# Second cross attention: norms and gate by ScalarE, statistics over three slots, last batch finished by halves

## What is computed

```python
def _L1_xattn_ref(x, latents, mask, kv_gate, ...):       # x: context [4, 1601, 256], latents: tokens [4, 512, 256]
    x = layernorm(x, gamma_media, beta_media)
    latents = layernorm(latents, gamma_lat, beta_lat)
    kv = concatenate((x, latents * kv_gate), axis=1)      # 2113 keys
    q, k, v = latents @ Wq, kv @ Wk, kv @ Wv              # 8 heads of 64
    sim = einsum(q * SCALE, k); sim = sim - max(sim)
    attn = softmax(where(valid, sim, -1e30))
    return einsum(attn, v) @ Wout
x = _layernorm(x + _L1_xattn_ref(ctx, x, mask, ...))      # then the experts, which first choose 2 of 8 by x @ gate_w
```

## Time and profile before

| | |
|---|---|
| median of 3 runs | 2418.3 us (2417.81 to 2419.02) |
| the profiled execution | 2418.87 us, its span 2417.1 us |
| busy | PE 2027.0, DVE 1616.6, ACT 1121.6, POOL 938.3 us |
| second cross attention | about 909 to 2057 us of the span |
| units 1 to 32, from one L2137 to the next | 968.9 to 2003.4 us |
| mean granted TensorE clock | 0.926 of full speed |

### The profile page before, as it was taken

One profiled execution on the slowest core, in us unless ns is written; L12 is line 12 of the kernel. 1 busy time (PEld: TensorE's weight loads), 2 busy tenths in 40 slices (PEclk: granted clock), 3 DMA queues, 4 the chain that ended last, 5 costly groups with the idle time before them and its releaser, 6 DMA issues. The chain is left out here.

```text
span 2417.1 us, 35796 instructions
## 1 busy us (share of the span) xinstructions
PE 2027.0 (84%) x12728; PEld 1406.0 (58%) x12728; DVE 1616.6 (67%) x2541; ACT 1121.6 (46%) x2142; POOL 938.3 (39%) x728
## 2 busy tenths in 40 slices
PE   7889849978899965877899799988899986599993
PEld 4556639962344444554566565655566564499992
DVE  5687745445878874888888877888788884322224
ACT  3333211103744653656666476656676672133332
POOL 3233232323113200455576456564576572222222
PEclk9999969988999987989999899999999998699997
DMA  3110035210000002000000000000000000531113
GB/s 148 37 37 21 10 144 206 91 57 18 1 1 1 0 1 90 1 1 1 28 1 1 10 28 1 1 10 1 1 1 1 10 1 9 221 134 36 38 34 113
DMA packets 36714, 93.29 MB, mean 39 GB/s; under 512 B 5415, under 2 KB 24379, under 8 KB 31934
## 3 DMA queue, kind: packets, MB, share of 16 engines
q1 hardware_dynamic: 30462, 74.72, 8.6%
q0 software_dynamic: 6080, 16.29, 2.0%
HBM read 76.56 MB, written 14.44 MB: 38 GB/s over the span
## 5 line engine op out<-in xcount | busy, mean ns | idle before, releaser
L1965 POOL TENSOR_TENSOR x_total<-x_total,x_pt 128x1024 f32<-128x1024 f32 x186 | 439.2, 2361 | 198.4 <-ACT x_pt L2024 182.4
L2045 ACT ACTIVATE x_pt<-PS,x_maskf 128x512 f32<-128x512 f32 x544 | 332.2, 687 | 180.8 <-PE PS L2313 177.8
L2127 DVE TENSOR_TENSOR PS<-x_pt,PS 128x512 f32<-128x512 f32 x480 | 333.2, 694 | 74.8 <-ACT x_pt L2045 36.8
L2284 PE MATMUL PS<-x_pt,x_vs 128*64 128x256 f32 x2176 | 286.1, 404 | 77.9 <-ACT x_pt L2024 72.1
L2145 DVE TENSOR_TENSOR x_pt<-x_pt,PS 128x1024 f32<-128x1024 f32 x320 | 320.4, 1051 | 0.7 <-PE PS L2331 0.7
L2024 ACT ACTIVATE x_pt<-x_pt 128x1536 f32<-128x1536 f32 (+1 forms) x160 | 266.1, 1664 | 50.6 <-DVE x_pt L2145 50.4
L2313 PE MATMUL PS<-x_qs,x_ks 64*128 64x256 f32 x2176 | 282.0, 395 | 1.9 <-ACT x_pt L2045 1.9
L2284 PEld LDWEIGHTS PS<-x_pt,x_vs 128*64 128x64 f32 x2176 | 153.8, 143 | 205.8 <-ACT x_pt L2024 78.0
L1143 PEld LDWEIGHTS PS<-m_xT,m_own 128*128 128x128 f32 x1984 | 235.5, 195 | 7.4 <-DVE m_own L1219 3.3
L1143 PE MATMUL PS<-m_xT,m_own 128*128 128x128 f32 x1984 | 236.4, 278 | 3.2 <-DVE m_own L1219 2.8
L2313 PEld LDWEIGHTS PS<-x_qs,x_ks 64*128 64x128 f32 x2176 | 199.5, 189 | 65.7 <-issue 40.2
(11 more groups left out here) (269 smaller groups left out, 2861.1 us busy)
## 6 DMA issues: line engine op xcount, KB each, us to landing
f_w<-in_L_ffn_w SPq DMA_DIRECT2D x32, 1024.0 KB, 6.3
a_ctxT<-in_ctxT SPq DMA_DIRECT2D x8, 800.5 KB, 4.4
f_w<-ys SPq DMA_DIRECT2D x24, 256.0 KB, 5.9
x_cx<-in_ctx SPq DMA_DIRECT2D x4, 1536.0 KB
l_w<-in_L_attn_w SPq DMA_DIRECT2D x6, 512.0 KB
a_xT<-in_xT SPq DMA_DIRECT2D x4, 512.0 KB, 5.2
X<-in_x SPq DMA_DIRECT2D x1, 2048.0 KB, 11.1
xr<-a_xn SPq DMA_DIRECT2D x16, 128.0 KB, 1.7
```

The source lines that it names most:

```text
L1965: ins = nc.gpsimd.tensor_tensor(total2[:], first, tile[:, 2 * k + 2:2 * k + 4, :], ALU.add)
L2045: nc.scalar.activation(pt[:, s % 2, t, :].rearrange("p (h n) -> p h n", h=2), PS[:, first:first + 2, half], ACT.Identity, bias=maskf[:, b ...
L2127: ins = nc.vector.tensor_tensor(acc, tile, acc, ALU.max)
L2284: mm = nc.tensor.matmul(PS[h * HDX:(h + 1) * HDX, AVB, 0:QN], vs[:, p % 2, t, h * HDX:(h + 1) * HDX], pt[:, u % 2, t, h * QN:(h + 1) * QN] ...
```

## The change

1. Norms by ScalarE. For b >= 1 `normalise` and the norm of the finished rows are ACT Identity activations with bias = -mean x rstd and scale = rstd, at the end of ACT's work of a group, in the same slots 3 and 4 (finished rows: slot 3, gi = 4). Batch 0's first norm stays with DVE. POOL's `rstd` and `rstd_out` get two small instructions each, for the bias.
2. `gate` is two ACT Copy activations, right behind the last N move (slot 6, gi = 4).
3. `stats` and `aggregate` go to slots 0, 1 and 2: 6, 6 and 5 tiles.
4. The loop ends with slot 32. What follows is written out: `weigh(31)` goes to bank 2, group by group as exponentials come; POOL adds up tiles 0 to 9 of unit 31 and PE the last 7; the O products are taken apart (`last_product`), with pairs 0 to 2 ahead of the last unit; residual, norm, transpose and logits go by halves, in banks of their own.

```diff
-        SLOTS = range(-1, UNITS + 6)
+        SLOTS = range(-1, UNITS + 1)
+        FINAL_AVB, FINAL_OUT, FINAL_TURN, FINAL_LOGITS = 2, (RB, 0), (1, 3), (ACC, AVB)
+        POOLED = 10
+                nc.gpsimd.tensor_scalar(nmu[:], mv[:, :, 0], -1.0, None, ALU.mult).then_inc(negated, 1)
                 pool.wait_ge(eps_added, b + 1)
+                if b >= 1:
+                    pool.wait_ge(ln_ready, b * NS)
                 nc.gpsimd.tensor_tensor(rs[:], ve[:], g["mhalf"][:].to_broadcast([P, NS]), ALU.pow).then_inc(rs_ready, 1)
+                pool.wait_ge(rs_ready, b + 1)
+                pool.wait_ge(negated, b + 1)
+                nc.gpsimd.tensor_tensor(shift[:], nmu[:], rs[:], ALU.mult).then_inc(shift_ready, 1)
...
+            u = UNITS - 1
+            for k in range(POOLED // 2 - 1):
+                add_up(u, k)
+            pool.wait_ge(summed, u * SUMS + POOLED // 2 - 1)
+            pool.wait_ge(av_done, u * NG)
+            nc.gpsimd.tensor_tensor(total[:], total2[:, 0, :], total2[:, 1, :], ALU.add).then_inc(summed, 1)
+            for half in range(2):
+                at = slice(2 * half, 2 * half + 2)
+                pool.wait_ge(mv2_ready, J * (B - 1) + 2 * half + 2)
+                nc.gpsimd.tensor_scalar(ve2[:, at], mv2[:, at, 1], LN_EPS, None, ALU.add).then_inc(eps2_added, 1)
+                pool.wait_ge(eps2_added, B + half)
+                nc.gpsimd.tensor_tensor(rs2[:, at], ve2[:, at], g["mhalf"][:].to_broadcast([P, 2]), ALU.pow).then_inc(rs2_ready, 1)
...
+                if use[0] == "N" and use == last_turn(use[1]):
+                    gate(use[1])
+
+            def gate(b):
+                act.wait_ge(moved, MOVED[last_turn(b)])
+                for k in range(KD):
+                    ins = nc.scalar.activation(kvT[:, b % 2, k, S2:KEYS], latT[:, k, :], ACT.Copy, scale=cols[:, 4 * KD:4 * KD + 1])
+                ins.then_inc(gated, 1)
+
+            def normalise(b, i):
+                src, dst, np_ = source(b, i)
+                if i == 0:
+                    act.wait_ge(shift_ready, b + 1)
+                nc.scalar.activation(dst, src, ACT.Identity, bias=shift[0:np_, i:i + 1], scale=rs[0:np_, i:i + 1])\
+                    .then_inc(ln_ready, 1)
...
+                    if exists(s) and s // UB + 1 < B and s % UB in (3, 4):
+                        at = (s % UB - 3) * NG + gi - 1
+                        for k in (2 * at, 2 * at + 1):
+                            if 0 <= k < NS:
+                                normalise(s // UB + 1, k)
+                    if UB <= s < UNITS and s % UB == 3 and gi == 4:
+                        b = s // UB
+                        act.wait_ge(shift2_ready, b)
+                        for j in range(J):
+                            x = X[:, (b - 1) * J + j, :]
+                            nc.scalar.activation(x, x, ACT.Identity, bias=shift2[:, j:j + 1], scale=rs2[:, j:j + 1])\
+                                .then_inc(x5_ready, 1)
+
+            exponent(UNITS - 1, NG - 1)
+            for half in range(2):
+                act.wait_ge(last_turned, half + 1)
+                if half == 0:
+                    act.wait_ge(ring_done, USE[("L", B - 2, 1)] + 1)
+                else:
+                    act.wait_ge(last_logits, 1)
+                nc.scalar.copy(x5T[:].rearrange("p j k n -> p (j k n)"), PS[:, FINAL_TURN[half], :]).then_inc(last_moved, 1)
...
+                avb = FINAL_AVB if u == UNITS - 1 else AVB
                 dve.wait_ge(av_done, u * NG + NG)
...
+            STATS = {at: range(at * NS // 14, (at + 1) * NS // 14) for at in range(14)}
-            dve.wait_ge(w_loaded, 16 * 6)
-            gate(0)
...
+                        for k in STATS.get(i * NG + gi, ()):
+                            counted[b + 1, k] = stats(b + 1, k)
+                        for k in STATS.get(i * NG + gi - 1, ()):
+                            aggregate(b + 1, k, counted[b + 1, k])
...
+            def last_residual(half):
+                dve.wait_ge(last_out, half + 1)
+                for i in range(2):
+                    x = X[:, (B - 1) * J + 2 * half + i, :]
+                    nc.vector.tensor_tensor(x, PS[:, FINAL_OUT[half], i * D:(i + 1) * D], x, ALU.add).then_inc(last_read, 1)
+                for i in range(2):
+                    j = 2 * half + i
+                    dve.wait_ge(last_read, 2 * half + i + 1)
+                    link(nc.vector.bn_stats(bn2[:, j, :], X[:, (B - 1) * J + j, :]))
+                    nc.vector.bn_aggr(mv2[:, j, :], bn2[:, j, :]).then_inc(mv2_ready, 1)
+
+            def last_norm(half):
+                dve.wait_ge(rs2_ready, B + half)
+                for j in (2 * half, 2 * half + 1):
+                    x = X[:, (B - 1) * J + j, :]
+                    nc.vector.tensor_scalar(x, x, mv2[:, j, 0:1], rs2[:, j:j + 1], ALU.subtract, ALU.mult).then_inc(x5_ready, 1)
+
+            def last_choice(half):
+                dve.wait_ge(last_logits, half + 1)
+                first = (B - 1) * J + 2 * half
+                nc.vector.tensor_copy(LG[:, first:first + 2, :],
+                                      PS[:, FINAL_LOGITS[half], 0:2 * E].rearrange("p (j e) -> p j e", e=E)).then_inc(LG_ready, 1)
+
+            last_residual(0)
+            weighted(UNITS - 1)
+            last_norm(0)
+            last_residual(1)
+            last_choice(0)
+            last_norm(1)
+            last_choice(1)
+            dve.wait_ge(LG_ready, 2)
...
+            def last_product(half, pairs):
+                for i in range(2):
+                    j = 2 * half + i
+                    for p in pairs:
+                        mm = nc.tensor.matmul(PS[:, FINAL_OUT[half], i * D:(i + 1) * D], o[:, p, j * P:(j + 1) * P], wo[:, p, :],
+                                              start=(i == 0 and p == 0), stop=(i == 1 and p == PAIRS_X - 1))
+                if pairs[-1] == PAIRS_X - 1:
+                    mm.then_inc(last_out, 1)
...
+                    if s == UNITS and gi == 0:
+                        released(pe, BY_NUMBER[-1])
+                        last_product(0, (0, 1, 2))
+                        pe.wait_ge(s_moved, UNITS * KT)
+                        last_product(1, (0, 1))
...
+            u = UNITS - 1
+            b, p, hq = unit(u)
+            pe.wait_ge(o_ready, u - 1)
+            last_product(1, (2,))
+            for gi in range(NG):
+                pe.wait_ge(exp_done, u * NG + gi + 1)
+                released(pe, ("V", b, p, gi))
+                for t in TILES[gi]:
+                    for h in range(2):
+                        nc.tensor.matmul(PS[h * HDX:(h + 1) * HDX, FINAL_AVB, 0:QN], vs[:, p % 2, t, h * HDX:(h + 1) * HDX],
+                                         pt[:, u % 2, t, h * QN:(h + 1) * QN], start=(t == 0), stop=False)
+            for t in range(POOLED, KT):
+                for h in range(2):
+                    nc.tensor.matmul(PS[h * HDX:(h + 1) * HDX, FINAL_AVB, QN:2 * QN], ones[:, 0:HDX],
+                                     pt[:, u % 2, t, h * QN:(h + 1) * QN], start=False, stop=False)
+            pe.wait_ge(o_ready, u)
+            last_product(0, (3,))
+            pe.wait_ge(summed, u * SUMS + POOLED // 2)
+            for h in range(2):
+                mm = nc.tensor.matmul(PS[h * HDX:(h + 1) * HDX, FINAL_AVB, QN:2 * QN], ones[:, 0:HDX],
+                                      total[:, h * QN:(h + 1) * QN], start=False, stop=True)
+            mm.then_inc(av_done, NG)
+            pe.wait_ge(o_ready, UNITS)
+            last_product(1, (3,))
+            for half in range(2):
+                pe.wait_ge(x5_ready, J * (B - 1) + 2 * half + 2)
+                for i in range(2):
+                    for k in range(KD):
+                        mm = nc.tensor.transpose(PS[:, FINAL_TURN[half], (i * KD + k) * P:(i * KD + k + 1) * P],
+                                                 X[:, (B - 1) * J + 2 * half + i, k * P:(k + 1) * P], ident[:])
+                mm.then_inc(last_turned, 1)
+                pe.wait_ge(last_moved, half + 1)
+                for i in range(2):
+                    for k in range(KD):
+                        mm = nc.tensor.matmul(PS[:, FINAL_LOGITS[half], i * E:(i + 1) * E], x5T[:, i, k, :], wg[:, k, :],
+                                              start=(k == 0), stop=(k == KD - 1))
+                mm.then_inc(last_logits, 1)
```

More of the change, by code:

```diff
@@ L2287, in weigh @@
                                                       start=(t == 0), stop=False)
[L2288 to L2294 removed]
+                        if gi == NG - 1:
                             pe.wait_ge(summed, (u + 1) * SUMS)
```

51 lines of the change are left out of this document (16 added, 35 removed).

## The result

The changed kernel takes 2316.1 us (median of 4 runs, 2314.09 to 2318.73) against 2418.66 us of the kernel before on the same chip (4 runs): ratio 0.9576, 95% interval 0.9564 to 0.9587. Its profiled execution took 2316.37 us with a span of 2314.6, so 102.5 us less span than before (2417.1). The forecast was 2320.6 us, its range 2298 to 2352.

What follows compares the result with a forecast made beforehand. An odd slot was taken to last as long as DVE's list plus the turn of the maxima through PE. Terms of 54.1 + 4.8 + 21.9 - 3.3 + 0 - 0.3 + 20.5 = 97.7 us gave 2320.6 us, range 2298 to 2352.

Steps and rivals of the forecast that it cites:

- slots 3 and 4, batches 0 to 2: Norms moved from DVE to ACT in these slots: 236.6 us become 182.5, 54.1 us gained.
- slots 27 and 28: Batch 3, where only the finished rows' norm leaves DVE: 63.09 us become 58.3, 4.8 gained (1 to 6).
- gate, slots 7: Gate ready before slot 7 begins: three slots fall from 34.6 to 27.3 us each, 21.9 gained (12 to 23).
- the end, with slot 31's 1.4: After the last exponential: last logits copied at 2036.4 instead of 2056.9, 20.5 us gained (14 to 24).
- the choice between the bounds: Slots 3 and 4, batches 0 to 2: gain from 30.6 us to 65.5; a value nearer the upper end taken.
- the rival in which all of it lies on the path: ACT becomes the bound, all its added work on the path: 25.5 us less gain, 2346 us; chance 0.22.
- 1.1 a slot, near two of 0.592: Slot 6: the gate's two ACT activations ahead of the score moves cost 1.1 us each slot, 3.3 lost (0 to 7).
- I charge 2 x 2.5 lost and 3 x 1.6 gained: Statistics: slots 0 of batches 1 and 2 lose 2.5 us each, slots 1 gain 1.6; net 0 (-5 to +5).
- not counted: the higher clock in slots that follow a pause: Slots that followed a pause before the change: a higher clock there, left out of the sum, no size given.
- The rival that PE works at half clock there: The end keeps its length: PE at half clock in the last 25 us, gain 10 not 20.5, 2331 us; chance 0.10.
- the case of all hidden: Rival: ACT's added work fully hidden, statistics in slot 0 free: 118.8 us gained, 2299.5 us; chance 0.13.
- The slower case: Rival: PE at half clock for whole slots 3 and 4, 27.7 us a slot; 2487 with all six; chance 0.04.

Runs made afterwards that it cites:

- e8: Changed kernel with a second ACT activation of the same size behind each of the 51 context and token norms, into a spare tile: 2334.85 us, 18.8 longer.
- e7: Changed kernel with ACT's context and token norms cut from 256 to 16 columns in batches 1 to 3: 2310.31 us, 5.8 shorter.
- e2: Changed kernel with the statistics put back to slots 1 and 2 of a batch, two tiles a group: 2323.21 us, 7.1 longer.
- e3: Kernel before with only the new end (and POOL's small bias operations, unused): 2402.19 us, 17.3 faster than before.
- e1: Changed kernel with the gate alone given back to DVE, at the start of slot 7: 2337.88 us, 21.8 longer.
- e10: Changed kernel with transposes and logits of the finished rows' second half moved from slot 5 to slot 7: 2306.65 us, 9.8 shorter.

## Why the prediction was right, point by point

The forecast of the sum was 97.7 us, the span shows 102.5. By terms, from the windows of the kernel before and of the two profiles of the changed kernel:

| term | forecast | measured | second profile |
|---|---|---|---|
| slots 3 and 4, batches 0 to 2 | 54.1 | 55.9 (236.6 to 180.8) | 52.6 |
| slots 27 and 28 | 4.8 | 4.9 | 4.9 |
| gate, slots 7 | 21.9 | 22.5 | 22.5 |
| gate, slots 6 | -3.3 | 0.0 | 0.0 |
| statistics, slots 0 to 2 | 0 | 3.6 | 4.0 |
| slots 5, batches 1 and 2 | not counted | -5.1 | -3.4 |
| start | -0.3 | -1.2 | 0.2 |
| the end, with slot 31's 1.4 | 20.5 | 21.5 | 20.5 |

The two columns of one program show how finely the terms can be read: to about 3 us for slots 3 and 4, to 1.6 for slots 5, to 1.4 for the start. Of slots 3 and 4 and of slots 5, 1.9 us is only the moved mark: cut at PE's turn of the maxima they are 54.0 and -3.2 (50.7 and -1.6 in the second profile).

*The reading of the bound held.* An odd slot lasts as long as DVE's list and the turn: slot 11 with DVE at 24.02 lasts 27.45 us. The price of ACT's norm (0.592 from the earlier trace rows, 0.60 to 0.62 measured) held, and so did the choice between the bounds. The split was a little off: slots 3 came at 27.5 instead of 28.4, since ACT's rest in the later groups was larger than the 2.3 us taken (in e8 eight activations more, 4.9 us, made these slots only 1.9 longer); slots 12 and 20 at 35.4 and 33.8 instead of 33.5, and at 35.3 and 37.0 in the second profile. There the wait at the start of slot 12 was half of the 2.9 charged (1.51 us), but the slot has a stretch at half clock (0.95). At full clock, slot 20 of the first profile, the even slot is what was forecast. e7 and e8 place ACT between the bounds as the prediction did: 4.2 of 10.7 us returned in e7, 18.8 of some 31 were paid in e8, and the rival in which all of it lies on the path gave 2346. Slot 28 was put at 30.3 for its start value, where the earlier trace rows have 30.56, and ACT's four activations cost it 0.6 instead of 1.0: two small errors that cancel.

*The gate.* Its gain was right. The step "1.1 a slot, near two of 0.592" failed: the form is dearer than that (2 x 0.716 = 1.4 us), and yet slots 6, 14 and 22 did not move by more than 0.01 us. ACT has 8 us of rest in them; the lower bound was the answer, and the reason that the prediction gave for it was the better one.

*The statistics.* The step "I charge 2 x 2.5 lost and 3 x 1.6 gained" oversized the loss and missed a gain: slots 8 and 16 lost 1.5 each, not 2.5; slots 1, 9 and 17 gained 1.6, 2.5 and 1.7; and slot 2, set at nothing although it gives up two tiles, gained 1.6, beside which DVE's work there fell by 0.8 (26.82 to 26.04) and PE's by 0.7 (31.85 to 31.13, clock 0.89 to 0.91). e2 puts the part at 7.1 in the medians and 6.4 in the slots 0 to 2 of its profile, against 3.6 and 4.0 between the two kernels: its slots 9 and 17 took 31.98 and 31.99, at a clock of 0.91, where the kernel before, with the same list, had 31.13 and 31.42 at 0.95. Between 3.6 and 7 is what these runs leave.

*The uncounted term.* The prediction left slots 5 out because nothing of theirs was moved, and as to the work that was right: cut at PE's turn of the maxima, slot 13 lasts 33.84 us before, and would after but for the clock. What it did not have is that one stretch more, behind two short rests, can run at the lower clock: 1.6 us in each of the two slots in the first profile; in the second, slot 21 had no more of it than before. What it set down as "not counted: the higher clock in slots that follow a pause" pointed the wrong way for these slots.

*The end.* 20.0 and 19.1 measured from the last reduction, 20.5 forecast, 19.1 alone in e3. The table's row also has slot 31, which the forecast did not name. The rival that PE works at half clock there is half true: four matmuls of L2353 at 1945.58 take 2.07 us instead of 1.13 and the last eight of L2468 1.88 instead of 1.06, which is 1.8 us, not 10.

*The start.* The -1.2 is scatter: the first reduction of maxima stands at 968.9 us before, at 970.1 and 968.8 in the two profiles of the changed kernel, and anywhere from 968.4 to 971.2 in the others.

*The range.* Its ends do not come out of the terms: the case of all hidden is worked out as 2299.5, not 2298, and ACT as the bound with the gate at 12 and the statistics at -5 is 2346 + 9.9 + 5 = 2361, not 2352. The measured time lies 18 and 36 us inside the stated ends, so nothing hung on it.

*The slower case* needed a slot at half clock throughout; the lowest granted clock of the changed kernel in slots 3 to 5 of any batch is 0.91 (slot 21, and slot 20 in the second profile). e8 shows its beginning: 0.88 in slot 12, which lasts 6.5 us longer.

The differences by the table are +1.8, +0.1, +0.6, +3.3, +3.6, -5.1, -0.9 and +1.0, together 4.4: 97.7 becomes 102.1 of the span's 102.5. That the total is off by 4.4 us where the single differences sum to 16.4 without their signs is in part luck: the uncounted slots 5 took back what gate and statistics gave beyond the forecast. The 54.0 against 54.1 of the main term is luck too, to about the 3 us by which two executions differ.

**What stays open.** What decides whether a stretch of PE behind two short rests runs at the upper or the lower clock: the same instructions with the same rests gave 33.83, 35.4 and 37.1 us for one slot, in different kernels, and 35.4 and 37.1 for slot 21 in two executions of the changed kernel. So it is not the program alone. e1's profile had all four slots at full clock; it is one execution of four, and whether anything in that kernel favours this is not shown.

## What to carry to other kernels

Where a VectorE `tensor_scalar` lasts several times its length at rest and ends together with a GpSimd instruction, its price is the neighbour's, and ScalarE may do it cheaper although its instruction is longer than VectorE's at rest; ask the engine's rest slot by slot for the cover. A short step that opens a stage (the gate) is worth moving for its place more than for its duration. After the repair, look at the slots *behind* the repaired ones: the short waits that stood there were worth 9.8 us (e10), more than the statistics, a whole part of the change. Run the same kernel twice before a slot's 1.6 us is given to an edit, and where slots are cut at an instruction of the engine that was relieved, cut them at another engine's as well: here the mark alone moved 0.9 us from one slot to the next.
